# Eight-layer hybrid network on one core: a 32-row spread of the normalisation factors, a PSUM bank for VectorE's FP4 operands, the state-space front in column chunks, and set-up work inside the local normalisations

## The reference

```
x = x + state_space(ln(x))        # left/right = x@W_up+b; conv of 3 taps, silu; delta = softplus(...);
                                  # B, C = x@W_B, x@W_C; scan over L with 64 states; gate; W_down
x = x + local_transformer(ln(x))  # 6 deep: qkv, l2norm, scaled rotary, windows of 32 + 32, 16 heads of 64,
                                  # out projection; layernorm, W1, gated gelu, W2
x = x + dense_attention(ln(x))
x = x + local_transformer(ln(x))  # the same weights
x = x + linear_attention(ln(x))
x = x + fp4_ffn(ln(x))            # blockwise FP4 of x, weights and h, below
x = x + head_attention(ln(x))
x = x + fp4_ffn(ln(x))

def fp4_quant_dequant(x):         # blocks of 16 along the last dim
    scale = max(max|xb| / 6, 1e-12)
    q = GRID[searchsorted(MID, |xb / scale|)] * sign(xb) * scale
fp4_ffn: h = silu(q(x) @ q(w_gate).T) * (q(x) @ q(w_up).T);  q(h) @ q(w_down).T
softplus(p) = max(p, 0) + ln(1 + exp(-|p|)), the kernel's form, with a correction of the rounding of 1 + e
```

## Time and profile before

| | us |
|---|---|
| median of 3 runs | 4401.29 (4400.63 to 4401.36) |
| the profiled execution's own time | 4401.53 |
| its span | 4399.7 |
| busy: PE, DVE, ACT, POOL | 3986.2, 3759.1, 3382.2, 3378.8 |
| mean granted TensorE clock | 0.952 |

### The profile page before, as it was taken

The page is one execution under the profiler, slowest core; times in us unless marked ns, Lnnn a source line. Parts: engine busy times, 40 slices in busy tenths (PEclk is TensorE's granted clock), DMA queues, the critical chain, the costliest instruction groups (busy, mean ns, idle before and its releaser), DMA issues. The chain is left out here.

```text
span 4399.7 us, 129691 instructions
## 1 busy us (share of the span) xinstructions
PE 3986.2 (91%) x45931; PEld 2638.4 (60%) x45931; DVE 3759.1 (85%) x12529; ACT 3382.2 (77%) x10674; POOL 3378.8 (77%) x4180
## 2 busy tenths in 40 slices
PE   5888789999999999999767999999999999986575
PEld 2333256777777767766553667777777677663353
DVE  5999779999999999999476999999999999965747
ACT  4888479999999999999414999999999999972121
POOL 2999688888888888888186888888888888842313
PEclk7999889999999999999887999999999999997787
DMA  1000100111111111011002111111111111000000
GB/s 27 1 1 1 45 23 24 46 32 26 50 26 43 36 33 46 24 33 31 11 2 56 27 26 50 26 41 38 33 37 34 41 36 33 24 23 3 5 3 10
DMA packets 77990, 121.96 MB, mean 28 GB/s; under 512 B 25832, under 2 KB 47012, under 8 KB 77348
## 3 DMA queue, kind: packets, MB, share of 16 engines
q1 hardware_dynamic: 77348, 113.71, 10.2%
HBM read 35.56 MB, written 1.05 MB: 8 GB/s over the span
## 5 line engine op out<-in xcount | busy, mean ns | idle before, releaser
L963 POOL TENSOR_TENSOR local_qk<-local_qk,local_rb 128x512 f32<-128x512 f32 x768 | 976.5, 1272 | 215.6 <-DVE local_rb L1353 201.4
L1233 ACT ACTIVATE local_pr<-local_tb,local_nmax 128x96 f32<-128x96 f32 x3072 | 997.7, 364 | 66.0 <-DVE local_nmax L1369 64.9
L1060 PE MATMUL local_pj<-local_wqkv,local_xs 128*128 128x512 f32 x1536 | 809.5, 620 | 37.0 <-DVE local_xs L1337 19.6
L969 POOL TENSOR_TENSOR local_qk<-local_qk,local_rinv 128x512 f32<-128x512 f32 x768 | 784.9, 1043 | 7.5
L1369 DVE CUSTOM_DVE_ANT_0 local_tb<-local_tb,local_mask 128x96 f32<-128x96 f32 x3072 | 688.8, 290 | 50.8 <-PE local_tb L1082 48.0
L1233 ACT ACTIVATION_READ_ACCUMULATOR local_pr<-local_tb,local_nmax 128x1 f32 x3072 | 706.1, 230 | 0.0
L985 POOL TENSOR_TENSOR local_pr<-local_pr,local_rsum 128x384 f32<-128x384 f32 x768 | 622.6, 827 | 36.9 <-DVE local_rsum L1375 36.9
L1350 DVE TENSOR_TENSOR local_qk<-local_pj,local_rope 128x512 f32<-128x512 f32 x768 | 523.7, 682 | 65.4 <-ACT local_sq L1216 46.0
L1216 ACT ACTIVATE local_sq<-local_pj 128x512 f32<-128x512 f32 x768 | 463.0, 628 | 134.1 <-PE local_pj L1060 129.2
L1353 DVE TENSOR_TENSOR local_rb<-local_pj,local_rope 128x512 f32<-128x512 f32 x768 | 523.2, 681 | 9.9 <-POOL local_qk L963 9.9
L1360 DVE TENSOR_REDUCE local_ss<-local_sq 128x8 f32<-128x512 f32 x768 | 512.2, 678 | 3.0 <-ACT local_sq L1216 0.8
(11 more groups left out here) (385 smaller groups left out, 7956.4 us busy)
## 6 DMA issues: line engine op xcount, KB each, us to landing
local_v<-local_v SPq DMA_DIRECT2D x288, 256.0 KB, 3.9
local_wqkv<-L_ffn_Wqkv_dram SPq DMA_DIRECT2D x72, 256.0 KB, 4.6
local_wo<-L_ffn_Wo_dram SPq DMA_DIRECT2D x12, 512.0 KB, 4.0
local_w<-L_ffn_W_dram SPq DMA_DIRECT2D x12, 341.0 KB, 4.8
mamba_parts<-mamba_in_low SPq DMA_DIRECT2D x12, 128.0 KB, 2.3
local_w<-L_ffn_W_dram SPq DMA_DIRECT2D x12, 128.0 KB
y_dram<-store_xtok SPq DMA_DIRECT2D x4, 256.0 KB, 2.5
local_oT<-rope_dram SPq DMA_DIRECT2D x2, 256.0 KB, 2.9
```

Source lines behind the costliest of these rows:

```text
L963: nc.gpsimd.tensor_tensor(qk[:, u, :], qk[:, u, :], rb[:, u % 2, :], ALU.add).then_inc(s["summed"], 1)
L969: nc.gpsimd.tensor_tensor(heads8(qk[:, u, :]), heads8(qk[:, u, :]), r, ALU.mult).then_inc(s["scaled"], 1)
L1060: nc.tensor.matmul(bank[:, :], xs[:, par, u // 4 * P:(u // 4 + 1) * P], wqkv[:, dep % 2, u % 4 * BANK:(u % 4 + 1) * BANK], start=True, sto ...
L1233: ins = nc.scalar.activation(pr[:, (NU * c + k) % PR_RING, i, WIN:WIN + KW], scores[:, i * KW:(i + 1) * KW], ACT.Exp, scale=-1.0, bias=nma ...
```

## The change

1. `normalise`: the variances are written at column 32 q + j, so that the inverse roots fill four groups of columns of a zeroed 128 x 128 tile. One transpose brings them onto partitions, ScalarE copies them, and 16 products of 32 rows by 128 columns with `net.pick` (made once at load) spread them, alternating between two banks. ScalarE copies z instead of VectorE. GpSimd and VectorE can be given work beside it.
2. `warm`: bf16 products of the identity with itself whose result nobody reads, 8 in each normalisation, and 10, 10, 6, 6, 6, 6 at the ends of the layers.
3. State-space front: casts, remainders and softplus by chunks, written in one interleaved order per engine; 24 DMAs for 12.
4. Local layers: masks, the first three tables, and VectorE's margins move into the normalisation; the stream is added per sequence.
5. FP4: VectorE's small operands and x's exponents move to a PSUM bank of its own, x is scaled a second time in place in PSUM, TensorE reads z directly and adds x by a product with the identity, ScalarE writes the sum back; all 11 iterations are written out.

The diff, cut to its core:

```diff
-def normalise(net, tag, prefetch):
+def warm(nc, net, bank, count):
+
+
+    for _ in range(count):
+        nc.tensor.matmul(bank, net.identb[:, :], view(net.identb[:, :], [[0, BANK // P], [1, P]]), start=True, stop=True)
+
...
+        GAP = P // NC
...
+        var = m.sb("var", [P, NC, NT])
+        root = [m.sb(f"root{i}", [P, P]) for i in range(2)]
+        tmp = [m.sb(f"tmp{i}", [P, NC, NT]) for i in range(2)]
+        rootT = m.sb("rootT", [P, P])
+        p_cen = m.ps("p_cen", [P, NC, BANK])
+        p_bc = m.ps("p_bc", [P, NC, BANK])
...
+            for r in root:
+                nc.gpsimd.memset(r[:, :], 0.0).then_inc(cleared, 1)
             for sem in net.past:
                 pool.sem_clear(sem)
+            if beside_pool:
+                beside_pool(pool)
...
+            def centre(q):
+                nc.tensor.matmul(p_cen[:, q, :], net.center[:, :], part(x, q), start=True, stop=True).then_inc(centred, 1)
+
+            def variance(q):
+                pe.wait_ge(squared, q + 1)
+                for j in range(NT):
+                    t, at = NT * q + j, GAP * q + j
+                    ins = nc.tensor.matmul(p_var[:, at:at + 1], sq[:, t * P:(t + 1) * P], net.mean[:, :], start=True, stop=True)
+                return ins
+
+            centre(0)
+            centre(1)
             for q in range(NC):
+                if q + 2 < NC:
+                    centre(q + 2)
+                ins = variance(q)
             ins.then_inc(summed, 1)
+            warm(nc, net, p_idle, 8)
+            pe.wait_ge(roots, 1 + ROOT_STEPS)
+            nc.tensor.transpose(p_rootT, root[1][:, :], net.ident[:, :]).then_inc(turned, 1)
+            pe.wait_ge(copied, 1)
+            for pair in ((0, 1), (2, 3)):
+                for j in range(NT):
+                    for q in pair:
+                        rows = slice(GAP * q, GAP * (q + 1))
+                        ins = nc.tensor.matmul(p_bc[:, q, j * P:(j + 1) * P], net.pick[rows, j, :], rootT[rows, :], start=True, stop=True)
+                ins.then_inc(spread, 1)
...
+            for q in range(NC):
+                nc.scalar.activation(part(z, q), p_cen[:, q, :], ACT.Copy)
+            act.wait_ge(turned, 1)
+            nc.scalar.activation(rootT[:, :], p_rootT, ACT.Copy).then_inc(copied, 1)
...
+            if beside_dve:
+                beside_dve(dve)
+            dve.wait_ge(summed, 1)
+            nc.vector.tensor_scalar(var[:, :, :], by_tile(p_var), LN_EPS, None, ALU.add).then_inc(roots, 1)
+            dve.wait_ge(cleared, 2)
+            dve.wait_ge(roots, 1)
+            inverse_root(nc, dve, roots, 1, var[:, :, :], [by_tile(r[:, :]) for r in root], [t[:, :, :] for t in tmp])
+            dve.wait_ge(copied, 1)
...
+                for own in range(2):
+                    cols_own = slice(own * T // 2, (own + 1) * T // 2)
+                    for k in range(3):
+                        sp.wait_ge(s[f"low{k}"], NQ // 2 * (own + 1))
+                        for half in range(2):
+                            for i in range(2):
+                                rows = slice(64 * i + 32 * half, 64 * i + 32 * half + 32)
+                                sp.dma_start(parts[i][32 * k:32 * k + 32, half, cols_own], low[k][rows, cols_own]).then_inc(s["parts_in"], 16)
+                sp.wait_ge(s["parts_in"], 16 * 24)
...
+    # ScalarE's order in the front, one call a line in the diff:
+    left_half(0); left_half(1); right_half(0); silu_x(0); left_half(2); right_half(1); silu_x(1); left_half(3);
+    right_half(2); biases(0); silu_x(2); cast(0, 0); right_half(3); biases(1); silu_x(3); cast(0, 1);
+    exponential(0); cast(1, 0); biases(2); exponential(1); cast(1, 1); cast(2, 0); cast(0, 2); biases(3); cast(2,
+    1); exponential(2); cast(0, 3); cast(1, 2); exponential(3); cast(2, 2); cast(1, 3); logarithm(0);
+    logarithm(1); cast(2, 3); logarithm(2); logarithm(3)
+    # VectorE's:
+    convolve(0); convolve(1); convolve(2); magnitude(0); convolve(3); remainder(0, 0); magnitude(1); remainder(0,
+    1); one_more(0); remainder(1, 0); magnitude(2); remainder(1, 1); one_more(1); remainder(0, 2); magnitude(3);
+    remainder(0, 3); remainder(1, 2); one_more(2); remainder(1, 3); one_more(3); for q in range(NQ):; steps(q)
...
+        EARLY_ROPES = 3
...
+            for k in range(EARLY_ROPES):
+                scaled_rope(k)
+
+        def prepare_margins(dve):
+            for i in range(2):
+                nc.vector.memset(xs[C // 2:C, i, 0:1], 0.0)
+            nc.vector.memset(xs2[C // 2:C, 0:1], 0.0)
+            nc.vector.memset(newton[:, :, :, 6], 1.5)
+
+            nc.vector.memset(v[0:QB, :, 3, :, :], 0.0)
+            nc.vector.memset(kT[:, :, :, 0:WIN], 0.0)
+            nc.vector.memset(pr[:, :, :, 0:WIN], 0.0).then_inc(s["pad_ok"], 1)
+
+        normalise(net, tag, prefetch, prepare_masks, prepare_margins)
...
-                    for k in range(1, DEPTH):
+                    for k in range(EARLY_ROPES, DEPTH):
                         scaled_rope(k)
 
-            scaled_rope(0)
             pipeline(pool, iteration, other_ropes)
 
...
+                if f >= SEQS - B:
+                    dve.wait_ge(s["z_ready"], B + f + 1)
+                    nc.vector.tensor_tensor(net.xT[:, f % B, :], net.xT[:, f % B, :], z[:, f % B, :], ALU.add)
...
-            dve.wait_ge(s["z_ready"], B + SEQS)
-            nc.vector.tensor_tensor(net.xT[:, :, :], net.xT[:, :, :], z[:, :, :], ALU.add)
...
+        x_in, x_back, h_last, p_out = p_x[:, 0:L], p_x[:, L:2 * L], p_last[:, 0:L], p_last[:, L:2 * L]
+
+        own = lambda at, width: p_own[:, at:at + width]
+        x_expo, x_am, x_inv0 = own(0, L), own(L, NX), own(L + NX, NX)
+        h_am, h_inv0, h_inv, h_scale = (own(L + 2 * NX + i * NHB, NHB) for i in range(4))
+        sx = {n: net.sem(f"{tag}_x_{n}") for n in ("am", "scale", "inv0", "inv", "a", "turned_a", "expo", "magic", "moved", "q", "out")}
...
+                nc.tensor.matmul(p_out, net.ident[:, :], net.xT[:, r, :], start=True, stop=False)
                 for j, rows in enumerate(DF_TILES):
-                    ins = nc.tensor.matmul(p_out[:, 0:L], net.w_down4[0:rows, j, :], hqT[0:rows, j, :], start=(j == 0), stop=(j == 2))
+                    ins = nc.tensor.matmul(p_out, net.w_down4[0:rows, j, :], hqT[0:rows, j, :], start=False, stop=(j == 2))
                 ins.then_inc(s["out_ready"], 1)
...
+            def add(r):
+                act.wait_ge(s["out_ready"], r + 1)
+                nc.scalar.activation(net.xT[:, r, :], p_out, ACT.Copy).then_inc(s["added"], 1)
...
+                done = n + 1
+                dve.wait_ge(s["z_turned"], done)
+                nc.vector.tensor_reduce(x_am, in_blocks(x_in), AX.X, ALU.max, apply_absolute_value=True).then_inc(sx["am"], 1)
+                need(dve, sx["out"], n)
+                dve.wait_ge(sx["am"], done)
+                nc.vector.tensor_scalar(x_["scale"][:, :], x_am, 1.0 / 6.0, 1e-12, ALU.mult, ALU.max).then_inc(sx["scale"], 1)
+                dve.wait_ge(sx["scale"], done)
+                nc.vector.reciprocal(x_inv0, x_["scale"][:, :]).then_inc(sx["inv0"], 1)
+                dve.wait_ge(sx["inv0"], done)
+                nc.vector.tensor_scalar(x_["inv"][:, :], x_inv0, TIES_DOWN, None, ALU.mult).then_inc(sx["inv"], 1)
+                dve.wait_ge(sx["inv"], done)
+                nc.vector.tensor_tensor(in_blocks(x_["a"][:, :]), in_blocks(x_in), per_block(x_["inv"][:, :]), ALU.mult).then_inc(sx["a"], 1)
+                dve.wait_ge(sx["a"], done)
+                nc.vector.tensor_tensor(in_blocks(x_in), in_blocks(x_in), per_block(x_["inv"][:, :]), ALU.mult).then_inc(sx["turned_a"], 1)
+                dve.wait_ge(sx["turned_a"], done)
+                nc.vector.tensor_scalar(x_expo.bitcast(U32), x_in.bitcast(U32), EXPONENT, None, ALU.bitwise_and).then_inc(sx["expo"], 1)
+                dve.wait_ge(sx["expo"], done)
...
+                nc.vector.tensor_scalar(h_scale, h_am, 1.0 / 6.0, 1e-12, ALU.mult, ALU.max).then_inc(sh["scale"], 1)
+                dve.wait_ge(sh["scale"], done)
+                nc.vector.reciprocal(h_inv0, h_scale).then_inc(sh["inv0"], 1)
+                dve.wait_ge(sh["inv0"], done)
+                nc.vector.tensor_scalar(h_inv, h_inv0, TIES_DOWN, None, ALU.mult).then_inc(sh["inv"], 1)
+                dve.wait_ge(sh["inv"], done)
+                nc.vector.tensor_tensor(in_blocks(h_["a"][:, :]), in_blocks(h[:, :]), per_block(h_inv), ALU.mult).then_inc(sh["a"], 1)
+                dve.wait_ge(sh["a"], done)
...
```

368 lines of the change are left out of this document (199 added, 169 removed).

## The result

The changed kernel takes 4340.08 us in the median (4336.77 to 4341.62, four runs) against 4400.96 (4398.60 to 4401.36): a ratio of 0.9862, 95% interval 0.9845 to 0.9879. Forecast were 4336 and a range of 4318 to 4360. Its profiled execution took 4341.62, with a span of 4339.8 against 4399.7: 59.9 us less where 65.2 were forecast.

The account below looks back on a forecast made before the run. Local transformers keep about 3,240 us; in the edited rest no engine is full. Normalisations -23.3, front -13.9, local starts -13.3, adds +2.0, FP4 -16.7 sum to -65.2: from 4401.53 to 4336 us, range 4318 to 4360.

Parts of the forecast that it names:

- Normalisations at full clock, 13.9: Each normalisation outside the local layers takes 13.9 us, the first 16.1, with fillers beside the roots: 85.6 against 114.3.
- rival (b): Normalisation spread: the 32-row products don't overlap, costing six times 1.4 us, total 4345; chance 0.15.
- Rival (c): Normalisations: fillers don't hold the clock but are still paid, so the normalisations give 0, total 4360; chance 0.07.
- Fillers at the ends, 6.9: Fillers at layers' ends hold the clock for the next centring but stand in the path: cost 6.9 us.
- Front, 38.4: State-space front, interleaved in 512-column pieces, ends at +38.4 us against +52.35: gain 13.9, bounds 33 and 42.
- rival (e): State-space front: interleaving makes new waits, 42 us instead of 38.4, total 4340; inside the forecast's own range.
- Local layers, -10.8: Two local layers, normalisation and body: 10.8 us less forecast, mainly from earlier margins and tables at their starts.
- rival (f): Local normalisations: root steps wait for GpSimd, 4.2 us each, +3.4 in all, total 4339; chance 0.2, inside the 0.60.
- The adds: Local layers' last sequences: eight more VectorE instructions of 0.45 us each, between 0 and 3.1 a layer, taken as +2.0 together.
- FP4, -16.7: FP4 layers: VectorE's period falls from 10.65 to 8.4, mean 9.1 with alternating clock; 8.35 us less a layer, 16.7 together.
- Rival (a): FP4 layers held by TensorE at the lower clock, period 10.8: +1.6 instead of -16.7, total 4354; chance 0.13.
- Rival (d): Slower: the local layers' 33 us period for each of 96 sequences lengthens; at 0.8 us a sequence, 4413; chance 0.03.

Follow-up runs that it names:

- run 4: Changed kernel plus one filler behind each of the first three groups of variance passes in every normalisation: 4337.7 us.
- run 2: Changed kernel without the fillers at the ends of six blocks, those inside the normalisations kept: 4342.6 us.
- run 12: Changed kernel with the former spread (scaled identity times ones, four products of 128 rows) instead of the transpose and 32-row products: 4339.8 us, ratio 0.9865.
- run 3: Changed kernel plus four fillers behind the spread in each normalisation: 4337.7 us.
- run 6: Changed kernel with FP4's second product of x left out and another order of ScalarE's and VectorE's work in the state-space front: 4341.1 us.
- 8: Changed kernel plus one filler behind each of the first three variance groups and four behind the spread: 4335.0 us.
- run 1: Changed kernel without the eight fillers inside each normalisation, those at the layers' ends kept: 4346.3 us.
- run 5: Changed kernel with FP4's block maxima of x and first inverse back in SBUF, and one early rotary table instead of three: 4373.3 us.
- run 9: Kernel of run 6 plus four fillers behind each FP4 down product, and GpSimd's early tables started behind the root steps: 4331.3 us.
- run 7: Changed kernel with all six rotary tables in the local normalisation and one add of the whole stream instead of eight by sequence: 4345.3 us.

## Why the prediction was right, and where its terms were off

**Normalisations at full clock, 13.9.** Right as worked out: run 4 has 14.4 with 0.38 us of extra fillers ahead of the sum. Two row groups do run side by side: 32 passes in 1.72 us, where 8 passes with as many columns took 3.67 at granted clock 1.00 and one after another they would take 3.4 (estimate: 8 at 0.43, the spacing of those), so rival (b) is excluded. The length of the fillers was right too: in run 2's first layer eight take 1.89 at 1.00, 0.38 for the last and 0.22 for each other. The term that failed is the cover: "eight bf16 fillers stand beside them" was to keep the clock. It fell before them, in the variances, in three of the six layers, and at the fillers in the other three. By the rows that is 1.2 us in each for the transpose and the first pair of banks, and in three of them 0.75 more ahead of the transpose and 0.8 to 1.0 on the variances: 12.1, less 2.2 since the first layer's centring found a clock higher than forecast: 9.8. Rival (c) had the cause in part; rival (b), whose cause didn't occur, had about the price, by chance.

**The new spread as a cause of gain.** It was credited within the normalisations. Run 12 shows that in this kernel, with its fillers, it is worth nothing measurable: with the former spread the same six normalisations took 94.4 us. Their gain comes from the rest of the edit: 5.0 us from the end fillers (run 2, 100.4 in the six), the other 14 from the order of centring and variances, z's copies on ScalarE and the fillers inside, which were not taken apart. Without the fillers inside, the former spread wasn't tried.

**Fillers at the ends, 6.9.** Their price was right in the first local layer (the next centring starts 4.26 us behind its last down product, 3.15 before) and put too high in the second (2.81, where 3.15 before; forecast was 1.0 more in each). They do hold the centring, but run 2 says that both sides are equal. The dense, linear and head bodies got 5.6 longer instead of 0.8 because the clock was low at their starts (run 3); the forecast had no term for the state in which a normalisation leaves TensorE.

**Front, 38.4.** Measured 41.4, inside its bound of 42 and nearly rival (e), but not for rival (e)'s reason. The lists laid side by side were right at full clock: in run 12, with the same lists and 1.00 in the first 12 us, the front took 38.5 and the first convolution came at +2.75. In the changed kernel that stretch had 0.76, and the convolution came at +4.56. The 3.0 us are again the low clock that the normalisation hands on. The two stalls of VectorE's list, 1.78 and 2.47, were forecast at 1.1 and 2.4. Each of ScalarE's three table loads took 1.28 us. The 24 loads of SyncE landed 2.0 us behind their issue in the median, the last of them, issued at 66.2, under the last steps (to 70.63). A better order is worth 2.2 to 2.3 on its own (run 6 against 3 and 8).

**Local layers, -10.8.** Measured -15.6. The starts were right: the first `recip` comes 7.1 and 8.8 us sooner, forecast 6.9 and 8.0. The local normalisations were to be closed by SyncE; VectorE's products closed them, since the root steps waited for GpSimd (rival (f), 0.2 us behind SyncE's end in the first, 0.4 in the second). Beside GpSimd's table instructions nine of the ten steps last 0.38 us where they last 0.17 without them, and in run 1 the tenth, the seed, lasted 4.02 in the first layer, until the tables' last instruction had ended, and the nine took 0.17. Run 5 (2.7 and 2.8 for the steps, with one table) and run 9 (2.33, with the tables behind them) show that the time of GpSimd's tables decides. Rival (f) put it at 4.2 in each layer, 1.7 of it behind SyncE, and the sum left it out; the cost is 1.9 to 3.8 on the chain, 0 to 2.9 behind SyncE. The adds were put too high: +2.0, where run 7 leaves no sum of that size. The rest, about 3 us, is within what these bodies vary by. The middle of the layers, from the first `recip` to VectorE's eighth-last sum into z, took 1387.7 and 1385.2 us before and 1385.1 and 1385.2 now, so the sign of being wrong that the prediction named there didn't show.

**FP4, -16.7.** The largest edit was the best understood: two stalls of 2.4 a period (run 5). The period came to 8.50 where VectorE decides (8.4 forecast) and a mean of 8.7 to 8.9 (9.1 forecast); the alternation between VectorE and TensorE that the forecast kept is there. The two x instructions that were to lose 0.13 each lost 0.14 and 0.13; the runs show this difference, not what the forecast named as its cause, and run 6 has 0.43 with only the output in PSUM. The product with the scale of h takes 0.88 where it took 1.09 (0.2 forecast). Off by more was the drain with its fillers: +2.6 forecast, 1.1 and 0.7 less measured. Rival (a) didn't come: the low half is 8.8 to 10.1, not 10.8 throughout. Rival (d) has nothing for it.

What stays open: why the low stretch of the clock falls at the start of the dense layer in runs 4 and 8 and not in run 3; its place differs between profiles of the same instructions (the state-space centring took 4.56 to 4.70 us in some runs and 6.3 to 6.9 in others), and no run here controls it.
